# Two transformer layers with routed experts on one core: one shared stage order in two routing rounds, against one order per engine in four rounds

## The reference

```python
xn = _layernorm(x)
x = x + _L0_attn_ref(xn, ...) + _L0_ffn_ref(xn, ...)
xn = _layernorm(x)
x = x + _L1_attn_ref(xn, ...) + _L1_ffn_ref(xn, ...)
# L0 attention: 16 heads of 8, biases, RMS norm of Q and K, softmax, sigmoid gate, output projection
# L0 ffn: shared expert (128 wide) + top 2 of 16 experts, 64 wide, silu(x Wg) * (x Wu) @ Wd, weights = probabilities
# L1 attention: 16 heads of 8, softmax, no output projection
# L1 ffn: top 2 of 8 experts, 352 wide, silu(x W1) * (x W3) @ W2, weights normalised to sum 1
```

## Time and profile before

| what | value |
|---|---|
| median of 3 runs | 921.08 us (915.45 to 922.29) |
| the profiled execution's own time | 915.65 us |
| its span, first to last instruction | 913.7 us |
| mean granted TensorE clock | 0.817 of full speed |
| PE, PEld, DVE, ACT, POOL busy | 73%, 35%, 55%, 46%, 33% of the span |
| DMA | 84.34 MB, mean 92 GB/s |

### The profile page before, as it was taken

The page is one execution under the profiler, slowest core; times in us unless marked ns, Lnnn a source line. Parts: engine busy times, 40 slices in busy tenths (PEclk is TensorE's granted clock), DMA queues, the critical chain, the costliest instruction groups (busy, mean ns, idle before and its releaser), DMA issues. The chain is left out here.

```text
span 913.7 us, 11538 instructions
## 1 busy us (share of the span) xinstructions
PE 670.5 (73%) x3578; PEld 318.7 (35%) x3578; DVE 498.9 (55%) x1050; ACT 421.5 (46%) x775; POOL 297.7 (33%) x403
## 2 busy tenths in 40 slices
PE   3154876776999998446798777688887878795576
PEld 1122332212344542212223221265555656551122
DVE  4178677744566677446677944443344443366551
ACT  1204545343677776223465433454444444454346
POOL 3305343365122124465300474221212212126430
PEclk9557786676899998667779876798888988899769
DMA  3182011033355422122110142334444344202120
GB/s 102 56 262 92 19 61 62 16 96 93 105 154 163 145 86 77 40 60 77 59 32 31 61 144 90 97 125 141 151 145 148 122 137 149 87 29 76 33 60 13
DMA packets 70827, 84.34 MB, mean 92 GB/s; under 512 B 7184, under 2 KB 58896, under 8 KB 70768
## 3 DMA queue, kind: packets, MB, share of 16 engines
q1 hardware_dynamic: 66672, 75.23, 26.6%
q0 software_dynamic: 4096, 8.40, 3.3%
HBM read 60.13 MB, written 23.46 MB: 91 GB/s over the span
## 5 line engine op out<-in xcount | busy, mean ns | idle before, releaser
L931 DVE TENSOR_REDUCE mx<-slot 128x1 f32<-128x512 f32 x512 | 331.0, 683 | 206.7 <-PE slot L555 156.1
L703 ACT ACTIVATE probsT<-slot 128x512 f32<-128x512 f32 x512 | 284.8, 597 | 223.4 <-PE slot L572 158.1
L572 PE MATMUL slot<-q_stack,k_stack 75*128 75x512 bf16 x512 | 215.2, 426 | 63.8 <-DVE mx L931 52.5
L555 PE MATMUL slot<-k_stack,q_stack 72*128 72x512 bf16 x512 | 218.3, 434 | 32.9 <-DMA k_stack<-parts_hbm 18.6
L584 PE MATMUL pv_ps<-probsT,v 128*32 128x512 f32 x1024 | 160.3, 702 | 2.7 <-issue 0.8
L1018 POOL TENSOR_TENSOR hid<-th,up 128x512 f32<-128x512 f32 (+2 forms) x46 | 58.3, 1268 | 228.3 <-DVE th L797 104.8
L555 PEld LDWEIGHTS slot<-k_stack,q_stack 72*128 72x128 bf16 x512 | 54.3, 106 | 177.7 <-issue 131.7
L533 PE MATMUL slot<-xgT,wbuf 128*128 128x128 f32 (+1 forms) x480 | 75.0, 322 | 36.9 <-DMA wbuf<-in_experts 36.9
L572 PEld LDWEIGHTS slot<-q_stack,k_stack 75*128 75x128 bf16 x512 | 53.7, 106 | 123.2 <-DVE mx L931 63.9
L533 PEld LDWEIGHTS slot<-xgT,wbuf 128*128 128x128 f32 (+1 forms) x480 | 72.0, 226 | 48.5 <-issue 46.1
L797 DVE SCALAR_TENSOR_TENSOR th<-th,slot 128x512 f32<-128x512 f32 (+2 forms) x46 | 31.4, 684 | 101.4 <-ACT th L658 80.5
(11 more groups left out here) (124 smaller groups left out, 598.8 us busy)
## 6 DMA issues: line engine op xcount, KB each, us to landing
wbuf<-in_experts SPq DMA_DIRECT2D x40, 544.0 KB, 5.3
q_stack<-parts_hbm SPq DMA_DIRECT2D x96, 96.0 KB
k_stack<-parts_hbm SPq DMA_DIRECT2D x96, 96.0 KB
parts_hbm<-parts SPq DMA_DIRECT2D x16, 384.0 KB, 2.5
wbuf<-in_experts SPq DMA_DIRECT2D x48, 128.0 KB, 2.1
xg<-xs_hbm SPq DMA_DIRECT2D x22, 256.0 KB, 3.2
ys_hbm<-ys SPq DMA_DIRECT2D x22, 256.0 KB, 2.7
xs_hbm<-zeros SPq DMA_DIRECT2D x1, 3072.0 KB, 15.1
```

Of the source, the lines that this page charges most:

```text
L555: nc.tensor.matmul(ps[:, 0:N], q_stack[0:STACK, h, j * P:(j + 1) * P], k_stack[0:STACK, h, :], start=True, stop=True).then_inc(slot_full, 1)
L572: nc.tensor.matmul(ps[:, 0:N], k_stack[0:STACK + MAXROWS, h, j * P:(j + 1) * P], q_stack[:, h, :], start=True, stop=True).then_inc(slot_fu ...
L703: nc.scalar.activation(probsT[:, k % PROBS, a, :], ps[:, 0:N], ACT.Exp, scale=SCALE).then_inc(slot_free, 1)
L931: nc.vector.tensor_reduce(mx[:, g, u // J, u % J:u % J + 1], ps[:, 0:N], AXIS.X, ALU.max)\
```

## The change

The order of each engine is now computed when the kernel is built, and the experts are worked in four rounds `r` (two in each layer, of two sequences, 1024 tokens each). `moments()` still holds wanted times, now only priorities. `tasks()` lists each stage once for each engine that has a part in it, with how long the engine is held, when the result is there, and the tasks that it needs. `engine_orders()` plays this forward: whenever an engine is free it takes, of its tasks whose needs are met, the one wanted first; PE also needs one of the 7 slots, and at most 3 are held by M and 3 by E at once (`AT_ONCE`). The order and the slots so found are fixed in the program; at run time the engines still wait for semaphores, in that order. The lengths given include M on DVE 0.62, E on ACT 0.51, PV 1.07, RF 3.4 of SP, SC and YG 1.96 of POOL for each tile, WL 1.15.

```diff
-Q = (12, 10)
-NB = (48, 40)
+TR = T // 2
+Q = (8, 6)
+NB = (32, 24)
+SETUP = (-3.0, -0.4, 2.2, 3.4, 10.0, 10.6, 14.0, 17.5)
+ROUTE = (1.5, 4.6, 11.8, 18.2)
+GROUPS = ((3.2, 0.45), (6.8, 0.45), (13.6, 0.8), (20.0, 1.0))
...
+            add(sp, ("RF", A, g), 3.4, 5.6, (sp, ("PW", A)), new and (pe, ("PV", A - 1, g, J - 1)), chain="RF")
+            for u in range(HG * J):
+                add(pe, ("M", A, g, u), 0.216, 0.45, u == 0 and (sp, ("RF", A, g)), chain="M")
+                add(dve, ("M", A, g, u), 0.62, 0.75, (pe, ("M", A, g, u)), chain="M")
+            add(pool, ("MP", A, g), 1.7, 1.75, (dve, ("M", A, g, HG * J - 1)), chain="MP")
...
+def engine_orders():
...
+    while True:
+        moved = True
+        while moved:
+            moved = False
+            for engine in ready:
+                if busy[engine] > now:
+                    continue
+                could = ready[engine]
+                if engine == "PE":
+                    could = [key for key in could if key[1][0] not in FILLS or
+                             open_slots and held.get(key[1][0], 0) < AT_ONCE.get(key[1][0], SLOTS)]
+                if not could:
+                    continue
+                key = min(could, key=lambda k: (found[k].wanted, number[k]))
+                ready[engine].remove(key)
+                task = found[key]
+                task.start = now
+                busy[engine] = now + task.holds
+                ends.append((now + task.lasts, key))
+                orders[engine].append(key[1])
...
-            for stage in plan.order:
+            for stage in plan.orders["PE"]:
...
-                    sp.dma_start(hbm["maxima"][A, g], mxT[:, g % 2, :]).then_inc(mx_out, 16)
-                    sp.wait_ge(mx_out, 16 * (A * G + g + 1))
-                    sp.dma_start(q_stack[STACK:STACK + MAXROWS, g * HG:(g + 1) * HG, :],
-                                 hbm["maxima"][A, g].rearrange("(a h) t -> a h t", h=HG)).then_inc(mx_in[g], 16)
+                    for a in range(MAXROWS):
+                        sp.dma_start(q_stack[STACK + a:STACK + a + 1, g * HG:(g + 1) * HG, :],
+                                     mxT[a * HG:(a + 1) * HG, g % 2, :]).then_inc(mx_in[g], 16)
...
-        qk_tok = xg[:].rearrange("p a b d -> p (a b d)")
+        qk_tok = sb("qk_tok", [P, J * 2 * D])
...
-                    if A == B:
-                        ve.wait_ge(scattered[0], 2 * T * 16)
+                    if A >= B and A % 2 == 0:
+                        ve.wait_ge(scattered[(A - B) // 2], 2 * TR * 16)
```

More of the change, by code:

```diff
@@ L134, in schedule @@
[L134 to L139, removed]
-    for s in range(B):
[L141 to L146, removed]
+                    put(t + 0.3 + 0.1 * c, "GG", r, q, c)
@@ new lines, in last_use, with buffer_of, __init__ @@
+def last_use(r, b):
+    l = r // 2
+    k = (r % 2) * NB[l] + b - WBUF[l]
+    if k >= 0:
+        return [("DN", 2 * l + k // NB[l], k % NB[l] // 4)]
+    return [("DN", 1, Q[0] - 1)] if l else []
+def buffer_of(r, b):
+    return ((r % 2) * NB[r // 2] + b) % WBUF[r // 2]
+class Task:
+    def __init__(self, engine, stage, wanted, holds, lasts, needs):
+        self.engine, self.stage, self.wanted = engine, stage, wanted
+        self.holds, self.lasts, self.needs = holds, lasts, needs
+        self.start = self.end = None
@@ new lines, in engine_orders @@
+def engine_orders():
+    found, gated = tasks()
+    waiting = {key: set(task.needs) for key, task in found.items()}
+    after = {key: [] for key in found}
+    for key, task in found.items():
+        for need in waiting[key]:
+            after[need].append(key)
+    ready = {engine: [] for engine in ("PE", "ACT", "DVE", "POOL", "SP")}
+    number = {key: k for k, key in enumerate(found)}
+    for key, left in waiting.items():
+        if not left:
+            ready[key[0]].append(key)
+    frees = {freer(stage): stage for engine, stage in found if engine == "PE" and stage[0] in FILLS}
+    busy = {engine: 0.0 for engine in ready}
+    ends = []
+    orders = {engine: [] for engine in ready}
+    ring, open_slots, held = {}, list(range(SLOTS)), {}
+    now = 0.0
+    while True:
[18 more added lines that the diff above has]
+                orders[engine].append(key[1])
+                if engine == "PE" and key[1][0] in FILLS:
+                    ring[key[1]] = open_slots.pop(0)
+                    held[key[1][0]] = held.get(key[1][0], 0) + 1
+                moved = True
+        if not ends:
+            break
+        later = [time for time in busy.values() if time > now] + [time for time, _ in ends]
+        now = min(time for time in later if time > now) if any(time > now for time in later) else now
+        done = [entry for entry in ends if entry[0] <= now]
+        ends = [entry for entry in ends if entry[0] > now]
+        for _, key in sorted(done):
+            found[key].end = now
+            if key in frees:
+                stage = frees[key]
+                open_slots.append(ring[stage])
+                held[stage[0]] -= 1
+            for other in after[key]:
+                waiting[other].discard(key)
+                if not waiting[other]:
+                    ready[other[0]].append(other)
+    left = [key for key, task in found.items() if task.end is None]
+    assert not left, left[:10]
+    return orders, ring, gated, found
@@ L610, in _ @@
             sc.wait_ge(first_in, 64)
-            for stage in plan.order:
+            for stage in plan.orders["ACT"]:
                 kind = stage[0]
@@ L732, in _ @@
             ve.wait_ge(x_in, 16)
-            for stage in plan.order:
+            for stage in plan.orders["DVE"]:
                 kind = stage[0]
@@ L961, in _ @@
             gp.wait_ge(consts_set, 4)
-            for stage in plan.order:
+            for stage in plan.orders["POOL"]:
                 kind = stage[0]
```

565 lines of the change are left out of this document (369 added, 196 removed).

## The result

The changed kernel takes 730.37 us (median of 4 runs, 728.87 to 739.85) where the kernel before took 919.94 (915.45 to 922.29): a ratio of 0.794, 95% interval 0.790 to 0.797. The forecast was 698 with 655 to 800. The profiled execution is one of the slower ones: it took 739.85 us with a span of 736.6 at a mean clock of 0.905, where the others have spans of 727 to 729 at 0.914 to 0.930, so about 9 us of its span belong to this execution alone.

A forecast was written before the change was run, and what follows sets the result against it. The prediction took the order of stages, not the work, as the bound. Start 49, middle (575 - 17) / 0.90 and tail 23 gave a span of 692 us, hence 698 us measured, with 655 to 800 for 8 in 10.

The forecast's parts named there:

- four signs: PE busy over 85%, mean clock above 0.93, ACT's and DVE's matmul waits under 70 us, first M before 52 us.
- PE's work, 575 us: PE's full-clock work over the whole kernel: 548 us before, plus 27 us for the added expert groups.
- The first M at 49.4: Start of the kernel: the first M matmul stays at 49.4 us, the first setup's chain being the same.
- The zeros: Start: zeros issued first, at about 10 us, 7.3 MB; first M up to 4 us later, taken as 0.
- The tail of 23 us: End of the kernel: 23 us remain after the last M result, as before; round 3 was held to have slack.
- The share of 0.90: Middle, between start and tail: the order lets PE work 0.90 of the time, against 0.63 before.
- Maxima past HBM, 1 to 3 us: Return of the maxima: one DMA round less in 32 groups, gaining 1 to 3 us in the last group only.
- The port, 5 us: DVE's additions at L833, lengthened by port sharing with GpSimd: a whole loss of 5 us, kept in the sum.
- The clock rival: PE's gaps keep the mean granted clock at 0.82 throughout: 811 us; chance 0.18 for 750 to 820.
- DVE as the bound of layer 0: Layer 0: DVE's 265 us at a share of 0.80 take 330 us, giving 737; chance 0.12.
- Head-of-line waits: PE waits in fixed order for maxima and weights, 246 us in 60 places: 944 us; chance 0.02, in part 0.03.
- Near the old order: Whole kernel: the computed orders come out near the old list's, some 860 us; chance 0.06.

The follow-up runs named there:

- e1: The changed kernel with its four rounds, but all engines again walk one common list sorted by wanted times: 888.53 us, ratio 0.966 to the kernel before.
- e2: The changed kernel's list scheduler, but two rounds of 2048 tokens and wanted times refitted: 832.27 us, ratio 0.904 to the kernel before.
- e8: The changed kernel run again without edit, on a chip where the kernel before takes 895 us: 706.84 us, ratio 0.789.
- e3: The changed kernel in its own orders, but the maxima go by way of HBM again, two DMAs with a wait between: 733.46 us, ratio 0.796.
- e4: The changed kernel in the same orders, but DVE takes each maximum over 256 of the 512 keys: 718.62 us, ratio 0.779.
- e7: The changed kernel, but the scheduler may begin sequence 1 only when sequence 0 is normalised, wanted times refitted: 734.99 us, ratio 0.820.
- e9: The changed kernel with routing in pieces and the traces' stage lengths given to the scheduler, wanted times refitted: 725.28 us, ratio 0.808.
- e6: The changed kernel, but on DVE the routing stages of rounds 1 to 3 are cut into pieces, other engines' orders kept: 701.09 us, ratio 0.784.

## Why the prediction was right, and where its sizes were off

The direction and the mechanism were right: the bound was the order, and PE's work over the share of it that an order reaches, between a start and a tail, is the time. 730.37 lies just above the prediction's inner range of 665 to 730 and 32 us above its 698. Of its four signs, one came (PE busy over 85% from 60 us on: 93%). The mean clock was 0.905 for "above 0.93", DVE's wait for M 130.5 us for "under 70" (ACT's 70.3), the first M at 56.6 for "before 52". The sum was 49 + 558 / 0.90 + 23 = 692; the profiled execution has 56.6 + 543 / 0.844 + 36.7 = 737. Term by term:

**PE's work, 575 us.** Measured 580. The rounds' 27 us of added work are there, and e1 and e2 show that they pay.

**The first M at 49.4.** It came at 56.6. The step said "since the chain of the first setup is the same": it is the same chain, but not with the same neighbours. The zeros, which the prediction names as the sign of a first M after 53 us, were not the cause. (They were 88 blocks of 64 KB before, 5.8 MB and not 5.6.)

**The tail of 23 us.** It is 36.7. The step "neither end grows" failed. It gave round 3 110 of 300 us and did not ask when in these 300 us the order puts its last group. The plan could have told that: played forward, `engine_orders()` itself has 43.7 us behind the last copy. From the last maximum to the last attention result it is 20.5 us before, 22.3 in e8 and 28.4 here; the two runs of eight gathers make it 36 in all in either profile. Since attention goes on beside these gathers, the ends are less of a loss than they look: PE does 38 us of work in them, not 17.

**The share of 0.90.** By the prediction's own method it was 0.84: 580 us of work less 38 in the ends, 543 us in 643. That method, busy time by the mean clock of the whole span, sets the work too low, since the clock is low where PE is idle. Summed over the stretches of either clock, the work is 564 us before, 589 here and 589 in e8, and the share of the middle is 551 / 643 = 0.86 here and 552 / 612 = 0.90 in e8. In the changed kernel's windows from 50 to 650 us, PE is idle for 54 us and loses 45 to the half clock; in e8, the same program on a chip of the other kind, these are 45 and 21. So of the 45 us between 692 and the span of 736.6, 8 are the start, 14 the tail and 23 the middle. The two ends are as long in e8 (55.9 and 36.7), but its middle is 8 us shorter than forecast: the step that was wrong on either kind of chip is the ends. Of the 23 us some 9 are this profile's distance from the median, and the rest goes with the chip. The slower kind shows it on ACT and DVE together:

```profile
344.91 1.31 ACT L976 ACTIVATE probsT<-slot 128x512 f32<-128x512 f32 x2 [4.09 <-remote]
```

```profile
344.21 1.43 DVE L1207 TENSOR_REDUCE mx<-slot 128x1 f32<-128x512 f32 x2 [3.24 <-remote]
```

Both stand still from 341 us on for nothing that the profile can name, though PE's results for them were there. PE then stands for 3.27 us, and the clock is at half from 344.1 to 354.4 us; how much of the difference between the two kinds of chip comes in this way was not tested. Such stops of 0.9 us and more behind 100 us sum to 23 us on ACT and 17 on DVE here, and in e8 to 1.3 and 0. The kernel before has waits of this kind as well, 58 and 49 us on the same engines, the longest 11 us.

**Maxima past HBM, 1 to 3 us:** e3 differs by 3.1 us, within the noise, so no more than that it is small is shown. **Weights** (2.4 us of waits in the up matmuls) were right. The 1.3 us of issue that the tail's estimate takes from the earlier trace rows is not in these rows.

**The port, 5 us.** The mean at L1106 is 461 ns in e8 for a median of 346: 64 x 0.115 = 7.4 us on DVE, so the sum was about right. But it was costed as DVE's time, and 5.3 of it lie in one place, where in the profile of after POOL ran six 128x512 operations and one of 64 rows without a break from 234.5 to 243:

```profile
236.28 7.63 DVE L1106 SCALAR_TENSOR_TENSOR x<-yg,w_ab,x 128x128 f32<-128x128 f32 x8
```

```profile
239.36 1.14 POOL L1263 TENSOR_TENSOR rest<-qk,parts 128x512 f32<-128x512 f32 x1
240.59 1.15 POOL L1264 TENSOR_TENSOR parts<-qk,parts 128x512 bf16<-128x512 f32 x1
```

The eight additions took 7.63 us against 2.31 at 714.92, where POOL stood idle, a maximum was late behind them, and PE stood 5.15 us; in e8's windows the half clock behind that takes 3.71 x 0.47 + 4.98 x 0.21 = 2.8 us more (245 to 250 us had PE busy 4.98 at 0.79): 8 us of PE for 5.3 of DVE. The Trainium skill, page "SBUF — State Buffer", section "Who interferes with whom", says that a DVE instruction with two SBUF inputs contends with a GpSimd instruction that reads SBUF, over a shared pair of ports that works as an exclusive lock. The trace agrees: of the five additions begun while POOL ran, one took 0.76 us and four 1.19 to 2.47, as long as one or two of POOL's 1.15, and the three begun behind POOL's last one took 0.34 each.

**The rivals.** The clock rival (mean granted clock stays at 0.82) fell: 0.905 here, 0.942 in e8. DVE as the bound of layer 0 fell with e4. Head-of-line waits fell: PE's gaps over 1 us sum to 36 us, of which the weights and the maxima hold a sixth, not 246. "Near the old order" fell with 730.

## What to carry to other kernels

Cutting work into smaller batches and freeing the engines' orders are worth little one without the other (31 and 88 us of 190 here): ask of either what it needs of the other. A list scheduler that never idles an engine lets ready work in ahead of the critical chain at the start and may leave the work with the longest chain behind it for the end; its own total did not rank plans within a few per cent of each other (663 for e7's and 666 for the changed kernel's, measured 28 us the other way; 702 and 732 in e9), so measure several, and read from the plan how long its first and last stretch are. And put the unchanged kernel beside every experiment of a few per cent: here the chip alone made 3%.

## What the runs showed of the hardware

Two kinds of chip were met: the kernel before took 895 us on two and 918 to 920 on others, the changed kernel 707 and 730. In the changed kernel on the slower kind PE, ACT and DVE show stops of 1 to 5 us that the profile puts down to nothing or to an unknown releaser, behind 100 us 8, 23 and 17 us in all; on the faster kind there are practically none (0, 1.3 and 0). Their cause was not tested.

The granted clock does not answer a gap alike each time. With PE almost fully busy behind a gap of 1.70 us it was at 1.2 GHz for 13.7 us in the changed kernel, 10.2 in e3 and 6.8 in e8, and a gap of 2.69 us in e6, with PE busy 6.84 of 10 us around it, left it at 2.4 GHz. An estimate that charges each gap the same is off by this much.
